# Dynamic convolution by pairs of heads in a small vision tower: one weight load for two heads, and a copy in two halves

## The reference, cut to what matters

```python
h = tok(x, W, b)                                  # 768 -> 256 features, 1024 tokens
h = layernorm(h + attn(h))
h = layernorm(h + ffn(h))                         # 256 -> 1024 -> 256, weights and activations quantised

def attn(x):                                      # x: (images, patches, 256)
    h = x @ w1.T + b1
    h = dynamic_conv(h)
    h = h @ w2.T + b2
    return layer_norm(x + h, gamma, beta)

def dynamic_conv(h):                              # 16 heads of 16 channels, 31 taps
    w = softmax((h @ ww.T + bw).reshape(T, B, 16, 31))
    hp = pad(h.reshape(T, B, 16, 16), 30 rows ahead in T)
    return sum over k of w[:, :, :, k:k+1] * hp[k:k+T]
```

## Time and profile before

| | |
|---|---|
| median of three runs | 127.28 us |
| span of the profiled execution, first to last instruction | 125.7 us |
| own time of the profiled execution | not given apart from its span; median less span is 1.6 us |
| TensorE matmuls busy | 107.9 us (86%) |
| VectorE busy | 86.1 us (69%) |
| GpSimd busy | 80.8 us (64%) |
| ScalarE busy | 66.1 us (53%) |
| the convolution's matmuls (line 417) | 256 records, 15.8 us busy |

### The profile page before, as it was taken

How to read it: one execution, slowest core, us unless ns; L and a number is a source line. 1 busy time by engine, 2 the same in 40 slices (tenths; PEclk the granted TensorE clock), 3 DMA queues, 4 the chain that set the end, 5 groups by cost and what they waited for, 6 DMA issues and landing times.

```text
span 125.7 us, 2379 instructions
## 1 busy us (share of the span) xinstructions
PE 107.9 (86%) x718; PEld 67.8 (54%) x718; DVE 86.1 (69%) x202; ACT 66.1 (53%) x109; POOL 80.8 (64%) x153
## 2 busy tenths in 40 slices
PE   6997999999999999999999999999998653884400
PEld 2673465866856486467555576668573322453200
DVE  5014593644965768799998999888696676898410
ACT  0042128639527444594633988766783836575200
POOL 6994000059700865867974868798888888888870
PEclk9999999999999999999999999999999999689975
DMA  3899999962321122232313112212300100011112
GB/s 104 260 357 340 399 420 422 400 255 21 63 24 17 42 25 23 53 51 42 32 42 30 14 42 25 22 42 27 64 0 0 42 0 0 4 46 42 44 43 82
DMA packets 23467, 12.45 MB, mean 99 GB/s; under 512 B 18141, under 2 KB 21981, under 8 KB 23070
## 3 DMA queue, kind: packets, MB, share of 16 engines
q1 hardware_dynamic: 21936, 10.46, 29.4%
q10 hardware_dynamic: 1518, 1.84, 4.8%
HBM read 9.95 MB, written 2.34 MB: 98 GB/s over the span
## 4 chain that ended last, share of the span: by engine, by line
PE 63%; POOL 19%; issue 5%; DMA 4%; ACTq 2%; DVE 2%; POOLq 1%
PE bank L339 12%; PE bank L417 11%; PE bank L400 11%; PE bank L383 6%; PE bank L444 5%; POOL q L1080 5%; DMA bias_cols<-in_cols 4%; PE bank L472 4%; PE bank L488 3%; POOL rstd L999 3%; POOL f L1087 3%; PE bank L357 3%; ACTq L676 2%; POOL res L1055 2%; POOL veps L998 2%
## 5 line engine op out<-in xcount | busy, mean ns | idle before, releaser
L339 PE MATMUL bank<-xT,tokW 128*128 128x256 f32 x72 | 16.7, 381 | 0.0
L417 PE MATMUL bank<-conv_w,vpad 128*32 128x128 f32 x256 | 15.8, 398 | 0.0
L1043 POOL TENSOR_TENSOR taps<-probs,inv_total 128x256 f32<-128x256 f32 x8 | 5.1, 634 | 15.7 <-DVE inv_total L741 15.4
L339 PEld LDWEIGHTS bank<-xT,tokW 128*128 128x128 f32 x72 | 13.5, 190 | 2.6 <-issue 0.9
L400 PE MATMUL bank<-wl,h1T 128*128 128x496 f32 x32 | 14.6, 578 | 0.0
L641 ACT ACTIVATE gu<-bank,sc 128x512 f32<-128x512 f32 x16 | 11.0, 686 | 5.3 <-PE bank L472 5.1
L527 PE MATMUL bank<-w_q,q2T 128*128 128x256 f16 x64 | 8.5, 273 | 3.9 <-ACT q2T L655 3.5
L812 DVE TENSOR_TENSOR gu<-gu,bank 128x512 f32<-128x512 f32 x16 | 10.8, 681 | 1.3 <-ACT gu L641 0.6
L998 POOL TENSOR_SCALAR veps<-mv 128x1 f32<-128x1 f32 x16 | 3.6, 225 | 11.9 <-DVE mv L751 10.9
L417 PEld LDWEIGHTS bank<-conv_w,vpad 128*32 128x32 f32 x256 | 8.3, 122 | 5.2 <-issue 1.4
L1080 POOL TENSOR_SCALAR q<-gu,sc 128x512 f16<-128x512 f32 x14 | 10.0, 716 | 1.4 <-DVE sc L829 0.2
(11 more groups left out here) (119 smaller groups left out, 237.2 us busy)
## 6 DMA issues: line engine op xcount, KB each, us to landing
xT<-in_xT SPq DMA_DIRECT2D x3, 768.0 KB, 16.9
w_raw<-in_wg SPq DMA_DIRECT2D x1, 1024.0 KB, 13.2
w_raw<-in_wu SPq DMA_DIRECT2D x1, 1024.0 KB, 15.2
w_raw<-in_wd SPq DMA_DIRECT2D x1, 1024.0 KB, 16.9
shear<-taps SPq DMA_DIRECT2D x8, 128.0 KB, 1.8
conv_w<-shear SPq DMA_DIRECT2D x64, 16.0 KB, 2.0
out_dram<-res SPq DMA_DIRECT2D x8, 128.0 KB
tokW<-in_tokW SPq DMA_DIRECT2D x6, 128.0 KB, 5.0
```

What stands on the lines that cost most here:

```text
L339: last = nc.tensor.matmul(ps_embed(pair, m), tokW[:, k, m * P:(m + 1) * P], xT[:, pair, k, :], start=(k == 0), stop=(k == KC_PATCH - 1))
L417: last = nc.tensor.matmul(ps_yT[j * SLOT:(j + 1) * SLOT, k, :], vpad[:, s, h, :], conv_w[:, s, :, h], start=(par == 0), stop=(par == 1))
```

## The change

- `vpad` goes; `v` holds the 256 value columns as they are. `out_v` becomes a plain copy.
- `conv(t)` has eight matmuls instead of sixteen. Each takes the 32 value columns of two heads as weights and both heads' columns of `conv_w` as 256 moving columns (two neighbouring elements, step 16). It yields for each pair of heads all four combinations of values and taps; `ps_yT` now fills bank 3, with the two heads' results interleaved.
- `out_yT` copies the columns of the even heads, all partitions. The new `pick_odd(t)` on VectorE then overwrites the partitions of the odd heads by predicate. The next `conv` and `project_out` wait for `picked_ok`, thus for both.
- `ps_q1T` moves to bank 0. `in_transposes` now waits for the last embed's copy and for `scaled_down`, and `embed` and `down` wait for `out_q1T`.
- The predicate: GpSimd writes an iota to `odd_head` between its first constants, and VectorE masks it. VectorE's memset of `vpad` goes.
- ScalarE's list: `out_h1T(3, 0)` ahead of `out_q1T(0)`, `scaled_down(2)` ahead of `out_q1T(5)`, `scaled_down(4)` ahead of `out_q1T(7)`. VectorE's list gets eight `pick_odd` calls.

```diff
-        vpad = sb("vpad", [P, SLOTS, HEADS, SLOT])
+        v = sb("v", [P, SLOTS, D])
+        odd_head = sb("odd_head", [P, 1], i32)
-        ps_yT = bank[3][:, 0:D].rearrange("p (k n) -> p k n", k=KC)
-        ps_q1T = bank[3].bitcast(f16)[:, 2 * D:3 * D].rearrange("p (k n) -> p k n", k=KC)
+        ps_yT = bank[3][:, :].rearrange("p (k n b) -> p k n b", k=KC, b=2)
+        ps_q1T = bank[0].bitcast(f16)[:, 2 * D:3 * D].rearrange("p (k n) -> p k n", k=KC)
...
 def embed(pair, m):              # the bank 0 branch
+                    if put["q1T"]:
+                        pe.wait_ge(q1T_ok, put["q1T"])
...
 def conv(t):
                 if t >= 1:
-                    pe.wait_ge(yT_ok, t)
-                if put["q1T"]:
-                    pe.wait_ge(q1T_ok, put["q1T"])
+                    pe.wait_ge(picked_ok, t)
                 for k in range(KC):
-                    for par in range(2):
-                        for j in range(QUADS):
-                            h = (k * QUADS + j) * 2 + par
-                            last = nc.tensor.matmul(ps_yT[j * SLOT:(j + 1) * SLOT, k, :], vpad[:, s, h, :],
-                                                    conv_w[:, s, :, h], start=(par == 0), stop=(par == 1))
+                    for j in range(QUADS):
+                        i = k * QUADS + j
+                        last = nc.tensor.matmul(ps_yT[j * SLOT:(j + 1) * SLOT, k], v[:, s, i * SLOT:(i + 1) * SLOT],
+                                                conv_w[:, s, :, 2 * i:2 * i + 2], start=True, stop=True)
...
 def project_out(t):
-                pe.wait_ge(yT_ok, t + 1)
+                pe.wait_ge(picked_ok, t + 1)
 def in_transposes(t):
-                if put["conv"]:
-                    pe.wait_ge(yT_ok, put["conv"])
+                pe.wait_ge(h1T_ok, put["embed0"])
+                if put["down"]:
+                    pe.wait_ge(down_read, put["down"])
 def down(t, half):
                     pe.wait_ge(h1T_ok, put["embed0"])
+                    pe.wait_ge(q1T_ok, put["q1T"])
...
 def out_yT(t):
-                nc.scalar.copy(yT[:, t % 2], ps_yT).then_inc(yT_ok, 1)
+                nc.scalar.copy(yT[:, t % 2], ps_yT[:, :, :, 0]).then_inc(yT_ok, 1)
...
+            def pick_odd(t):
+
+                dve.wait_ge(yT_ok, t + 1)
+                nc.vector.copy_predicated(yT[:, t % 2], odd_head[:].unsqueeze(2).broadcast_to([P, KC, P]),
+                                          ps_yT[:, :, :, 1]).then_inc(picked_ok, 1)
...
-            nc.vector.memset(vpad[:], 0.0).then_inc(zeros_ok, 1)
+            dve.wait_ge(place_ok, 1)
+            nc.vector.tensor_scalar(odd_head[:], odd_head[:], R, None, ALU.bitwise_and).then_inc(odd_ok, 1)
+            dve.wait_ge(odd_ok, 1)
...
+            nc.gpsimd.iota(odd_head[:], pattern=[[0, 1]], base=0, channel_multiplier=1).then_inc(place_ok, 1)
```

More of the change, by code:

```diff
@@ L204, in vit_tower @@
         inv_ok = sem("inv_ok")
[L205 removed]
+        odd_ok = sem("odd_ok")
+        picked_ok = sem("picked_ok")
         attn_read = sem("attn_read")
@@ L586, in out_v @@
                 act.wait_ge(v_ps, t + 1)
-                if t == 0:
-                    act.wait_ge(zeros_ok, 1)
                 if t >= SLOTS:
                     act.wait_ge(yT_ps, t - SLOTS + 1)
-                nc.scalar.copy(vpad[:, t % SLOTS].rearrange("p (a b) (c r) -> p a (b c) r", b=2, c=2)[:, :, 0:4:3, :],
-                               ps_v.rearrange("p (a b r) -> p a b r", b=2, r=R)).then_inc(v_ok, 1)
+                nc.scalar.copy(v[:, t % SLOTS], ps_v).then_inc(v_ok, 1)
             def exps(t):
@@ L687, in _ @@
             out_h1T(2, 1); out_h1(0); exps(3); out_yT(0); out_v(1); weight_finish(1); out_h1(1); exps(4)
-            out_yT(1); centre(0); out_v(2); quant_in(0); out_q1T(0); out_h1T(3, 0); out_h1(2); centre(1)
+            out_yT(1); centre(0); out_v(2); quant_in(0); out_h1T(3, 0); out_q1T(0); out_h1(2); centre(1)
             exps(5); out_yT(2); nc.scalar.preload_act_table(ACT.Silu); silus(0, 0); quant_in(1); out_v(3)
@@ L695, in _ @@
             scaled_down(1); out_q1T(4); out_v(7); silus(4, 0); quant_in(5); out_h1(7); silus(4, 1); out_q2T(2)
-            out_yT(7); centre(6); out_q1T(5); scaled_down(2); silus(5, 0); quant_in(6); out_q2T(3); silus(5, 1)
-            out_q1T(6); scaled_down(3); silus(6, 0); centre(7); out_q2T(4); silus(6, 1); quant_in(7); out_q1T(7)
-            scaled_down(4); silus(7, 0); out_q2T(5); silus(7, 1); scaled_down(5); out_q2T(6); scaled_down(6)
+            out_yT(7); centre(6); scaled_down(2); out_q1T(5); silus(5, 0); quant_in(6); out_q2T(3); silus(5, 1)
+            out_q1T(6); scaled_down(3); silus(6, 0); centre(7); out_q2T(4); silus(6, 1); quant_in(7); scaled_down(4)
+            out_q1T(7); silus(7, 0); out_q2T(5); silus(7, 1); scaled_down(5); out_q2T(6); scaled_down(6)
             quant_last_half(); out_q2T_last()
@@ L955, in _ @@
             top_logits(2); shift(2); weight_clip(1, wclip_up); top_logits(3); shift(3); tap_sums(2)
-            tap_inverses(2); tap_sums(3); tap_inverses(3); attn_stats(0); attn_variance(0); attn_centre(0)
-            top_logits(4); shift(4); attn_norm(0); mid_stats(0); mid_variance(0); weight_scales(2, 3)
+            tap_inverses(2); tap_sums(3); tap_inverses(3); pick_odd(0); attn_stats(0); attn_variance(0); attn_centre(0)
+            top_logits(4); shift(4); attn_norm(0); mid_stats(0); mid_variance(0); pick_odd(1); weight_scales(2, 3)
@@ L958, in _ @@
             mid_absmax(0); attn_stats(1); attn_variance(1); mid_scales(0); out_scales(0); attn_centre(1)
             attn_norm(1); mid_stats(1); mid_variance(1); tap_sums(4); tap_inverses(4); top_logits(5); shift(5)
-            mid_absmax(1); mid_scales(1); out_scales(1); tap_sums(5); tap_inverses(5); attn_stats(2)
+            mid_absmax(1); mid_scales(1); pick_odd(2); out_scales(1); tap_sums(5); tap_inverses(5); attn_stats(2)
             attn_variance(2); attn_centre(2); inner(0, 0); attn_norm(2); mid_stats(2); mid_variance(2)
@@ L962, in _ @@
             inner(0, 1); mid_absmax(2); inner_absmax(0); mid_scales(2); out_scales(2); inner(1, 0)
-            inner_scales(0); down_scale(0); inner(1, 1); inner_absmax(1); inner_scales(1); down_scale(1)
+            inner_scales(0); down_scale(0); inner(1, 1); pick_odd(3); inner_absmax(1); inner_scales(1); down_scale(1)
             top_logits(6); shift(6); attn_stats(3); attn_variance(3); inner(2, 0); attn_centre(3); attn_norm(3)
             mid_stats(3); mid_variance(3); inner(2, 1); top_logits(7); tap_sums(6); tap_inverses(6)
-            mid_absmax(3); shift(7); mid_scales(3); out_scales(3); inner_absmax(2); attn_stats(4)
+            mid_absmax(3); pick_odd(4); shift(7); mid_scales(3); out_scales(3); inner_absmax(2); attn_stats(4)
@@ L967, in _ @@
             attn_variance(4); attn_centre(4); inner_scales(2); down_scale(2); attn_norm(4); out_stats(0)
-            out_variance(0); mid_stats(4); mid_variance(4); inner(3, 0); mid_absmax(4); tap_sums(7)
+            out_variance(0); mid_stats(4); mid_variance(4); inner(3, 0); mid_absmax(4); pick_odd(5); tap_sums(7)
             tap_inverses(7); mid_scales(4); out_scales(4); inner(3, 1); attn_stats(5); attn_variance(5)
-            attn_centre(5); inner_absmax(3); attn_norm(5); mid_stats(5); mid_variance(5); inner_scales(3)
+            attn_centre(5); inner_absmax(3); pick_odd(6); attn_norm(5); mid_stats(5); mid_variance(5); inner_scales(3)
@@ L971, in _ @@
             down_scale(3); mid_absmax(5); attn_stats(6); attn_variance(6); attn_centre(6); mid_scales(5)
-            out_scales(5); out_stats(1); out_variance(1); inner(4, 0); attn_norm(6); inner(4, 1); mid_stats(6)
+            out_scales(5); out_stats(1); out_variance(1); inner(4, 0); attn_norm(6); inner(4, 1); pick_odd(7); mid_stats(6)
             mid_variance(6); inner_absmax(4); mid_absmax(6); inner_scales(4); down_scale(4); attn_stats(7)
```

5 lines of the change are left out of this document (3 added, 2 removed).

## The result

The changed kernel takes 129.22 us (median of four runs, 128.56 to 129.64) against 127.17 us for the kernel before (four runs); the ratio is 1.0155, with a 95% interval of 1.0095 to 1.0215. It is slower by about 2 us, and the forecast was 128.8 us. The profiled execution, the longest of the four, took 129.64 us at a span of 127.8 us, where before had a span of 125.7 us.

A forecast was written before the change was run, and what follows sets the result against it. The end was taken as GpSimd's last wait, for tile 4's variance at 76.64 us, plus a constant. That row's +1.35 us and the start's +0.2 gave +1.55, so 127.28 became 128.8 us; 8-in-10 range 126.5 to 130.3 us.

The forecast's parts named there:

- What conv gains: Each convolution on TensorE, with 16 records in place of 32, saves 0.87 us; bounds 0 and 0.87 us.
- The pick: pick_odd on VectorE takes 0.45 us, between 0.37 and 0.68; ScalarE's copy keeps its 0.37 us.
- Steps 1 to 6: Walk from conv(0) to conv(3) and its pick: late picks and bank 0 waits put tile 3's variance at +1.4 us.
- step 4: conv(2) ends 0.2 us early, but pick_odd(2) queues behind the logits(5) chain: project_out(2) at 54.6 us, +0.5.
- Step 7: Tile 3 to 76.64 us: pick_odd(4) adds 0.45 us, attn_norm(3) perhaps freed gives -0.5; tile 4's variance at +1.35 us.
- The start: The iota ahead of GpSimd's conv_w memset delays b1_rep and the kernel's start by 0.2 us.
- From span to median: The 1.6 us between span and median stay, so 127.28 us becomes 128.8 us.
- Behind 76.64 us: After GpSimd's last wait, late convolution gains, three picks (1.35 us) and bank 0 waits (0.4 to 0.9 us each) change nothing.
- TensorE stays the bound: Rival: copies return in time, only two bank 0 waits are new; end at -1.5 us, 125.8 us; chance 0.17.
- The waits cancel: Rival: attn_norm(3) wholly freed and one of steps 4 to 6 is 0.5 us shorter; +0.45, 127.7 us; chance 0.13.
- The pass isn't faster: Rival: 256 columns still run at 1.7 ns each, convolution costs as before; +1.0 us more, 129.8 us; chance 0.13.
- The pick is held by GpSimd: Rival: picks 3 and 4 on VectorE each take 0.5 us more beside GpSimd; +2.6, 129.9 us; chance 0.12.

The follow-up runs named there:

- e7: Kernel before, but each convolution matmul reads its 128 moving columns side by side instead of with a step of 16 elements (wrong taps); one run, 124.68 us.
- e8: Changed kernel, but the two moving columns of a pair lie 8 elements (32 bytes) apart instead of neighbours (other heads' taps); one run, 131.57 us.
- e6: Changed kernel with TensorE's list reordered to cover two bank 0 waits, weight_finish(2) ahead of inv_std_attn(3), pick_odd(0) ahead of tap_sums(3); 126.61 us, ratio 0.9969 to before.
- e11: Changed kernel with only weight_finish(2) moved ahead of inv_std_attn(3) in GpSimd's list; 128.39 us, ratio 1.0126 to before.
- e10: Kernel before, without pairs or picks, with weight_finish(2) ahead of inv_std_attn(3) and VectorE's list rearranged between tiles 3 and 5; 126.86 us, ratio 1.0007.
- e1: Kernel before plus only the move of ps_q1T to bank 0 with its waits and ScalarE's new order; 128.37 us, ratio 1.0102.
- e4: Kernel before with only weight_finish(2) moved ahead of inv_std_attn(3) in GpSimd's list; 126.73 us, ratio 0.9969.
- e3: Changed kernel without the eight pick_odd calls, conv and project_out waiting for ScalarE's copy alone; 126.61 us, ratio 0.9975 to before.

## Why the prediction was right, step by step

The forecast was +1.55 us; measured are +2.0 us, for the causes that it named, with one term of the sum of the wrong sign. At GpSimd's row of tile 4 the +2.02 us are 0.13 of start, 1.09 up to tile 3 and 0.80 from there to tile 4, for which the forecast had 0.2, 1.4 and -0.05. So the total is nearer than its parts, by luck: the forecast had 0.3 us too much up to tile 3 and 0.85 us too little behind it.

- *What conv gains* was put at 0.87 us each. Over the eight it is (15.8 - 8.9) / 8 = 0.86 us. e7 and e8 show that the reason is whether reads in a row lie side by side. That agrees with the rule of the Trainium skill (SBUF — State Buffer, Specifications (TRN2)) on 16-byte lines, which must be hit at least twice; the width of 16 bytes itself no run here shows.
- *The pick* was put at 0.45 us and takes 0.44. ScalarE's copy was put at 0.37 and takes 0.35 to 0.38.
- *Steps 1 to 6.* Forecast and measured starts: `project_out(0)` 39.4 and 39.42; `project_out(1)` 45.35 and 45.39; `in_transposes(0)` 49.5 and 49.72; `project_out(2)` 54.6 and 54.74; `embed(3, 1)` 58.1 and 58.48; `inner(1, 1)` 63.65 and 64.08 us. The forecast's times leave out the start, which is 0.13 us of each difference; the rest goes from -0.1 to 0.3 us. (In step 4 the terms give 54.7, not 54.6.) The variance of tile 3 was put at +1.4; GpSimd gets it at +1.22 us, though `inner(1, 1)` comes at +1.64 and the pick behind it moves the next start by 0.35 more. Ahead of `top_logits(6)` 0.7 us were made good and not the 0.2 counted: besides the 0.19 us of idle time, `down_scale(1)`, an operation on one element with two SBUF inputs, took 0.58 us before, from 64.75 us to the end of GpSimd's `quant_inner` at 65.33, and takes 0.16 us in the changed kernel. That this covered the lateness of the steps ahead is luck.
- *Step 7* failed. I counted -0.5 us because VectorE might reach `attn_norm(3)` ahead of GpSimd's `weight_finish`. GpSimd started at 69.68 us and VectorE at 69.80: it lost by 0.12 us and was held for 2.05 us, where it had been held for 1.61. The term was +0.44 and not -0.5, and 0.8 us from tile 3 to tile 4 are the pick's 0.45 with it, within 0.1. Where two engines race for the same moment, both outcomes belong in the sum with their prices, and half of a gain is the one value that can't come.
- *The start* was put at +0.2, by way of the iota and `b_rep`. The iota took 0.13 us and `b_rep` ended 0.08 us later, at 10.93. But that isn't what the first convolution hangs on in these two profiles: it stands 22.07 and 22.05 us behind a cast of the bias row, which waits for a DMA (below). So its +0.13 us goes with the DMA, and the mechanism of this term is not borne out here. Where the bias row lands early, two kernels with the iota start their first convolution at 35.53 us (e6, e11) and two without at 35.43 and 35.44 us (e10, e1): 0.1 us at the most.
- *From span to median* the forecast kept 1.6 us. That took a median and the span of another run; where both are known, a run is 1.7 to 2.2 us longer than its own span. It doesn't change the +1.55 us.
- *Behind 76.64 us* nothing changed: 44.7 us in both. The three late convolutions, three picks and four waits on bank 0, of 1.03 to 1.64 us each, are all hidden behind GpSimd, as said. The forecast had named three of them at 0.4 to 0.9 us; `in_transposes(4)`, and `in_transposes(3)` with 0.94 us ahead of that row, were not in it.
- *The rivals.* "TensorE stays the bound" falls as the account of the whole, but e4 shows that it sits within 0.6 us of VectorE in the stretch that decides, and in e10 it is what VectorE waits for: nearer than I gave it. "The waits cancel" falls with step 7, where `attn_norm(3)` was held longer instead of freed. "The pass isn't faster" isn't the case; e8 plays it, and its one run, 131.57 us, is 1.9 us over the longest of the changed kernel, twice the 1.0 us I had worked out. "The pick is held by GpSimd": its eight records take 384 to 458 ns, so no. The third, at 54.24 us, lies wholly inside a GpSimd operation of 1.97 us on an SBUF tile and takes 0.44 us. That agrees with the rule of the Trainium skill (SBUF — State Buffer, SBUF: two separate sides) that a VectorE instruction with at most one SBUF input doesn't contend with GpSimd.

## What to carry to other kernels

A busy engine isn't the bound; find the last engine that never waits, go back to the last input that it waited for, and price every edit at that row. When an edit frees one engine and adds a handover through two others, walk the handover through their lists: here four convolutions saved 3.5 us, six new waits on TensorE took 3.1 us of idle time and `conv(3)` still came 1.6 us later. Three moved calls brought more than half of the loss back. Before dropping a faster operation, refit the lists to it, and refit the old kernel's lists too, and compare the best of both (0.9912 against 0.9969 here, where the old one had less fitting).

## What the runs showed of the hardware

A moving operand of float32 read with a step of 64 bytes (before, records of 128 columns) or of 32 bytes (e8, 256 columns) costs 1.8 ns a column; side by side, all of it (e7) or in pairs of neighbours (changed), it costs 0.9 ns. These come from the convolution's length less the mean length of a record, by the steps in between: (1.98 - 0.40) / 7 / 128, (2.03 - 0.64) / 3 / 256, (1.08 - 0.28) / 7 / 128 and (1.07 - 0.39) / 3 / 256. I had not expected it to be so clean, nor that twice the weight loads cost nothing: 1.08 us with 32 of them (e7), 1.07 with 16 (changed).

A predicated copy on VectorE of 256 float32 elements from PSUM, with its mask in SBUF, takes 0.38 to 0.46 us, also beside GpSimd. A VectorE operation with two SBUF inputs of 256 elements took 0.48 us in e4, and 1.61 (before), 1.95 (e3) and 2.05 us (changed) where it started after GpSimd's `weight_finish` of 1.90 us.

The start of the first convolution lay between 35.43 and 36.63 us. VectorE's waits for the bias row in e1 and e3, the earliest and the latest of the thirteen, show one source:

```profile
13.00 0.42 DVE L937 CAST bias_part<-bias_row 65x512 bf16<-65x512 f32 x1 [2.15 <-DMA bias_row<-in_bias]
```

```profile
14.57 0.42 DVE L942 CAST bias_part<-bias_row 65x512 bf16<-65x512 f32 x1 [3.65 <-DMA bias_row<-in_bias]
```

The bias row's cast starts up to 1.6 us apart, and the chain moves with it: wherever this cast starts at 13.49 us or later, in nine of the thirteen profiles, the first convolution follows it by 22.05 to 22.07 us. Where it starts at 13.37 us or earlier, the first convolution stays at 35.43 to 35.53 us, so there something else is last. `b_rep` ends between 10.82 and 10.94 us in all of them. Kernels that differ only later than this, such as before and e1, lie up to 0.9 us apart, so it isn't the edits: two single profiles can't be compared to better than about a microsecond without taking a common start off.
